# Expert layers of a top-2 mixture: tiles of 256 rows, with the first layer's weights as the stationary operand

## The reference, cut to what matters

```python
def _L1_ffn_ref(x, Wr, W1, b1, W2, b2):          # x: 32 x 96 x 192, F = 768, 8 experts
    x_flat = x.reshape(T, D)                     # T = 3072 rows
    gate_logits = x_flat @ Wr
    topw, topi = jax.lax.top_k(gate_logits, TOP_K)        # 2 of 8
    topw = jax.nn.softmax(topw, axis=-1)
    combine = jnp.zeros((T, N_EXPERTS), dtype=x.dtype)
    combine = combine.at[jnp.arange(T)[:, None], topi].add(topw)
    h = jax.nn.relu(jnp.einsum('td,edh->eth', x_flat, W1) + b1[:, None, :])
    y = jnp.einsum('eth,ehd->etd', h, W2) + b2[:, None, :]
    out = jnp.einsum('te,etd->td', combine, y)
    return out.reshape(B, S, D)
```

## Time and profile before

| what | value |
|---|---|
| time, median of 3 runs | 940.69 us (938.2 to 941.06) |
| span of the profiled execution | 938.0 us |
| the median less that span | 2.7 us |
| TensorE busy over the span | 770.3 us, 82% |
| VectorE / ScalarE / GpSimd busy | 553.9 / 424.6 / 362.2 us |
| first to last TensorE work of `expert_tiles` | 670.36 to 923.37 us |

### The profile page before, as it was taken

One profiled execution on the slowest core, in us unless ns is written; L12 is line 12 of the kernel. 1 busy time (PEld: TensorE's weight loads), 2 busy tenths in 40 slices (PEclk: granted clock), 3 DMA queues, 4 the chain that ended last, 5 costly groups with the idle time before them and its releaser, 6 DMA issues. The chain is left out here.

```text
span 938.0 us, 23848 instructions
## 1 busy us (share of the span) xinstructions
PE 770.3 (82%) x8368; PEld 648.7 (69%) x8369; DVE 553.9 (59%) x1400; ACT 424.6 (45%) x1069; POOL 362.2 (39%) x392
## 2 busy tenths in 40 slices
PE   3689999999977766556789999815599999999993
PEld 3578888888865543334557778604599999999993
DVE  2698887887742221111667777679555565556562
ACT  4667667677632211111125776445144444444441
POOL 1423434434320000000114788218755555555552
PEclk9999999999965987878669999855599999999997
DMA  9419000000026999999155000054123333333331
GB/s 256 111 47 429 33 2 2 2 2 3 2 102 194 422 423 426 426 425 396 28 237 240 1 2 1 1 146 103 59 45 53 50 54 50 49 49 49 53 50 17
DMA packets 34090, 118.16 MB, mean 126 GB/s; under 512 B 7570, under 2 KB 24372, under 8 KB 29524
## 3 DMA queue, kind: packets, MB, share of 16 engines
q1 hardware_dynamic: 23156, 104.30, 29.3%
q0 software_dynamic: 10848, 12.67, 8.4%
HBM read 105.77 MB, written 11.14 MB: 125 GB/s over the span
## 5 line engine op out<-in xcount | busy, mean ns | idle before, releaser
L1835 POOL DMA_INDIRECT out_h<-x_ys,idx x55 | 87.5, 1591 | 98.2 <-ACT x_ys L1860 93.2
L1959 PE MATMUL psum<-w_pairs,x_h_hi 128*128 x330 | 101.8, 371 | 1.2 <-DVE x_h_lo L1887 1.1
L1961 PE MATMUL psum<-w_pairs,x_h_lo 128*128 x330 | 82.6, 250 | 0.0
L1887 DVE TENSOR_TENSOR x_h_lo<-psum,x_h_hi 128x384 fp32r<-128x384 f32 x110 | 56.3, 553 | 39.0 <-ACT x_h_hi L1856 39.0
L521 POOL TENSOR_SCALAR a_u<-flat,a_mv 96x192 f32<-96x192 f32 x32 | 24.2, 757 | 133.9 <-DVE a_mv L693 133.9
L1860 ACT ACTIVATE x_ys<-x_ys,cw 128x192 f32<-128x192 f32 x55 | 25.1, 456 | 102.2 <-DVE x_ys L1898 102.2
L1856 ACT ACTIVATE x_h_hi<-psum 128x384 fp32r<-128x384 f32 x110 | 48.1, 489 | 37.6 <-PE psum L1948 35.8
L1959 PEld LDWEIGHTS psum<-w_pairs,x_h_hi 128*128 128x128 f32 x330 | 61.9, 188 | 3.5 <-issue 3.4
L1961 PEld LDWEIGHTS psum<-w_pairs,x_h_lo 128*128 128x128 f32 x330 | 62.9, 191 | 0.0
L1822 POOL DMA_INDIRECT x_xg<-xtab,idx x55 | 55.1, 1002 | 16.6 <-issue 16.1
L1208 PE MATMUL psum<-flat,yT 64*32 64x384 f32 x576 | 41.0, 639 | 24.9 <-issue 23.9
(11 more groups left out here) (284 smaller groups left out, 2264.8 us busy)
## 6 DMA issues: line engine op xcount, KB each, us to landing
flat<-in_slot_w SPq DMA_DIRECT2D x24, 2304.0 KB, 27.4
ring<-in_slot_w SPq DMA_DIRECT2D x8, 2304.0 KB, 29.7
flat<-in_moe_w SPq DMA_DIRECT2D x1, 10752.0 KB, 29.6
flat<-in_x_patches SPq DMA_DIRECT2D x4, 1536.0 KB, 14.2
out_h<-flat SPq DMA_DIRECT2D x1, 2304.0 KB, 12.1
xtab<-flat SPq DMA_DIRECT2D x4, 576.0 KB, 4.0
m_y<-in_fc_b SPq DMA_DIRECT2D x4, 384.0 KB, 7.4
x_xg<-xtab,idx POOLq DMA_INDIRECT x55
```

Source lines behind the costliest of these rows:

```text
L1835: pool.indirect_dma_start(out=A["out"][:, :], out_offset=bass.IndirectOffsetOnAxis(ap=g.idx[:, i:i + 1], axis=0), in_=ys[:, i % 2, :], in_ ...
L1887: v.tensor_tensor(h_lo[:, 3 * n:3 * n + 3, :], b_hT[n], h_hi[:, 3 * n:3 * n + 3, :].bitcast(F32), ALU.subtract).then_inc(s_hl, 1)
L1959: pe.matmul(b_y[u % 2], h_hi[:, k, :], g.w_pairs[:, :, k, bass.ds(e, 1), :].rearrange("p two a d -> p two (a d)"), start=(k == 0), stop=False)
L1961: mm = pe.matmul(b_y[u % 2][:, 1, :], h_lo[:, k, :], g.w_pairs[:, 1, k, bass.ds(e, 1), :].rearrange("p a d -> p (a d)"), start=False, stop ...
```

## The change

- `expert_tiles` takes 31 tiles of 256 rows (`NTB`), all of them always; a tile is two halves of 128 rows, so the lists have 62 columns (`NTILES`).
- In the first layer the weights are the stationary operand, a block of 128 features at a time, and x moves, 256 columns. So the features stand on the output's partitions, as the second layer needs them, and nothing is transposed in between. There are six groups `first(k)` of five matmuls, each into one of three PSUM banks, and six groups `second(k)`; they alternate.
- ScalarE makes relu's high part of a group, VectorE the low part in one scalar-tensor-tensor operation (`relu_rest`).
- The additions, the weighing and the scatters are done by halves. Scatters go ten halves behind the gathers; one waits for both halves of the tile before.
- The split first-layer weights no longer stay in SBUF for the products. attention1 stores them into a table in DRAM, `w1tab` (five DMAs, 12.4 MB, one of them of 62 partitions; `route` writes the bias rows), and SyncE fetches a tile's part, 1.573 MB, into one of four buffers, as soon as the first layer of the tile four before is done. The load of `b2` stands behind the first of them.

```diff
-NTILES = 55
+MT = 256
+NPAD = 256
+NWB = 4
+NTB = 31
+NTILES = 2 * NTB
...
+            for first, (low, high) in ((2, (2, 3)), (0, (0, 1))):
+                done = NE if first else 2 * NE
+                sp.wait_ge(g.s_hi, done)
+                sp.wait_ge(g.s_lo, done)
+                if first:
+                    sp.wait_ge(g.s_top, NE)
+                for m in (low, high):
+                    for rows in ((slice(0, 64), slice(66, 128)) if m == 3 else (slice(0, 128),)):
+                        sp.dma_start(A["w1tab"][:, rows, m * F:(m + 1) * F].rearrange("e p f -> p e f"),
+                                     g.w1_parts[m][rows, :, :].bitcast(F32)).then_inc(g.s_w1d, 16)
...
+            sp.wait_ge(g.s_w1d, 5 * 16)
+            sp.wait_ge(g.s_b1r, 32)
+            for i in range(NTB):
+                e = sp.value_load(g.te[0:1, i:i + 1], min_val=0, max_val=NE - 1)
+                if i >= NWB:
+                    sp.wait_ge(s_h1, (i - NWB + 1) * FC)
+                sp.dma_start(g.w1_buf[i % NWB].bitcast(F32), A["w1tab"][bass.ds(e, 1), :, :].rearrange("a p (m f) -> p (a m) f", m=4)
+                             ).then_inc(g.s_w1[i % NWB], 16)
+                if i == 0:
+                    sp.dma_start(b2[:, :, :], A["moe_b2"].unsqueeze(0).broadcast_to([128, NE, D])).then_inc(s_b2, 16)
...
-                i = t - 4
+                i = t - BEHIND
                 if i >= 0:
                     pool.wait_ge(s_ys, i + 1)
-                    if i >= 1:
-                        pool.wait_ge(s_add, 16 * i)
+                    if i >= 2:
+                        pool.wait_ge(s_add, 32 * (i // 2))
...
-            steps(act, NTILES, [(relu, 1), (x_copy, 0), (turn_copy, 1), (weigh, 2)])
+            steps(act, NTB, [(relu(0), 1), (relu(1), 1), (x_copy, 0), (weigh(0), 3), (relu(2), 1), (weigh(1), 3),
+                             (relu(3), 1), (relu(4), 1), (relu(5), 1)])
...
+            def relu_rest(k):
+                def stage(i, u):
+                    v.wait_ge(s_hh, i * FC + k + 1)
+                    v.scalar_tensor_tensor(h_lo[:, k, :], b_f[k % NF1], 0.0, h_hi[:, k, :].bitcast(F32),
+                                           ALU.max, ALU.subtract).then_inc(s_hl, 1)
+                return stage
...
-            steps(v, NTILES, [(relu, 1), (x_rest, 0), (turn_rest, 1), (add_bias, 2)])
+            steps(v, NTB, [(add_bias(0), 3), (relu_rest(0), 1), (relu_rest(1), 1), (x_rest, 0), (add_bias(1), 3),
+                           (relu_rest(2), 1), (relu_rest(3), 1), (relu_rest(4), 1), (relu_rest(5), 1)])
...
+            def first(k):
+                def stage(i, u):
+                    w = g.w1_buf[u % NWB]
+                    cols = slice(128 * k, 128 * k + 128)
...
+                    if not isinstance(i, int) or i * FC + k >= NF1:
+                        pe.wait_ge(s_hl, i * FC + (k + 1 - NF1))
+                    terms = ((x_hi, 0, 0, 128), (x_hi, 0, 1, 128), (x_lo, 0, 1, 128), (x_hi, 1, 2, 128), (x_lo, 1, 3, 66))
+                    for m, (x, c, part, rows) in enumerate(terms):
+                        mm = pe.matmul(b_f[k % NF1], w[0:rows, part, cols], x[0:rows, u % 2, c, :],
                                        start=(m == 0), stop=(m == len(terms) - 1))
                     mm.then_inc(s_h1, 1)
...
-            steps(pe, NTILES, [(pick, 0), (transpose_x, 0), (second, 2), (turn, 1), (first, 0)])
+            steps(pe, NTB, [(pick, 0), (first(0), 1), (second(0), 2), (first(1), 1), (second(1), 2), (transpose_x, 0),
+                            (first(2), 1), (second(2), 2), (first(3), 1), (second(3), 2), (first(4), 1), (second(4), 2),
+                            (first(5), 1), (second(5), 2)])
```

More of the change, by code:

```diff
@@ L178, in build @@
         g.s_add = sem("s_add")
+        g.s_w1d = sem("s_w1d")
+        g.s_w1 = [sem(f"s_w1_{i}") for i in range(NWB)]
         g.s_ring = [sem(f"s_ring{i}") for i in range(NU)]
@@ L1915, in expert @@
                 return pe.snap(regs[u], min_val=0, max_val=NE - 1)
[L1917 to L1918 removed]
             def transpose_x(i, u):
[L1921 to L1924 removed]
+                at = 2 * (u % 2)
+                for half in range(2):
+                    if isinstance(i, int):
+                        pe.wait_ge(s_x[at + half], 16 * (i // 2 + 1))
+                    else:
+                        pe.wait_ge(s_x[at + half], (i - u) * 8 + (16 * (u // 2) + 16))
@@ L1951, in second @@
-            def second(i, u):
-                if isinstance(i, int) and i == 0:
-                    pe.wait_ge(g.s_lo, n_early + len(on_pool))
-                    pe.wait_ge(s_lo_v, len(on_vector))
-                e = expert(u)
-                reused(pe, s_ya, i, 2)
-                for k in range(FC):
-                    pe.wait_ge(s_hl, i * 2 + k // 3 + 1)
-                    pe.matmul(b_y[u % 2], h_hi[:, k, :], g.w_pairs[:, :, k, bass.ds(e, 1), :].rearrange("p two a d -> p two (a d)"),
-                              start=(k == 0), stop=False)
-                    mm = pe.matmul(b_y[u % 2][:, 1, :], h_lo[:, k, :], g.w_pairs[:, 1, k, bass.ds(e, 1), :].rearrange(
-                        "p a d -> p (a d)"), start=False, stop=(k == FC - 1))
-                mm.then_inc(s_y, 1)
@@ L1965, in _, with second, stage @@
-            steps(pe, NTILES, [(pick, 0), (transpose_x, 0), (second, 2), (turn, 1), (first, 0)])
+                return stage
+            def second(k):
+                def stage(i, u):
+                    if isinstance(i, int) and i == 0 and k == 0:
+                        pe.wait_ge(g.s_lo, n_early + len(on_pool))
+                        pe.wait_ge(s_lo_v, len(on_vector))
+                    e = expert(u)
+                    if k == 0:
+                        reused(pe, s_ya, i, 2, 2)
+                    pe.wait_ge(s_hl, i * FC + k + 1)
+                    for half in range(2):
+                        part, bank = slice(128 * half, 128 * half + 128), b_y[u % 2][half]
+                        pe.matmul(bank, h_hi[:, k, part],
+                                  g.w_pairs[:, :, k, bass.ds(e, 1), :].rearrange("p two a d -> p two (a d)"),
+                                  start=(k == 0), stop=False)
+                        mm = pe.matmul(bank[:, 1, :], h_lo[:, k, part], g.w_pairs[:, 1, k, bass.ds(e, 1), :].rearrange(
+                            "p a d -> p (a d)"), start=False, stop=(k == FC - 1))
+                    mm.then_inc(s_y, 1)
+                return stage
```

202 lines of the change are left out of this document (93 added, 109 removed).

## The result

The changed kernel takes 958.45 us, the median of four runs (955.06 to 965.03), against 939.45 of the kernel before: a ratio of 1.0212 (1.0178 to 1.0246). That is 19 us slower, where 4 us faster had been forecast, and over the upper end of the range, 953. Each ratio in what follows is against executions of the kernel before that ran beside it, and leaves out executions over 1.5% slower than the fastest of the same kernel (three of ten in k1_store64, none elsewhere).

A forecast was written before the change was run, and what follows sets the result against it. The prediction took TensorE alone to pace the expert stage. Its terms, -13 us for TensorE, +7 up to the first matmul and +2 after the last, summed to -4: 936.7 us, with a range of 8 in 10 from 926 to 953.

The forecast's parts named there:

- TensorE, per tile: Expert stage: a tile of 256 rows takes 7.59 us, the stage 239.7 against 253.0, a gain of 13 us.
- rival B: First layer: matmuls of 256 columns run at the floor, 0.11 us each, 7 us better, 929; chance 0.17.
- the formula that the prediction quoted: Trainium skill, TensorE matmuls: columns / 2.4 GHz plus 2.5 ns, 109 ns at 256 columns; 8 us more gained, 929.
- the 0.20 for waits and the loop's edge: TensorE's tile in the expert stage: 0.20 us beyond matmuls and transposes, added unchanged to 7.39 to give 7.59.
- The tail: After the last matmul: two last scatters instead of one, one more issue with its gap, 1.9, taken as +2 us.
- rival D: VectorE in the expert stage: relu_rest queued behind other work delays TensorE, a tile at 7.9, +9 us, 946; chance 0.11.
- The front: Sorting stage up to the first matmul: longer list, extra cast, second gather and wider first operations, +7 us (bounds +5 and +9).
- counted as nothing: Attention stage: storing the split weights into DRAM, 12.4 MB, 29 us at 426 GB/s, was put at no cost.
- rival E: Weight stores to DRAM: 62 partitions on two engines make sorting-stage stores up to 19 us late; half, +9, 946; chance 0.10.
- list and cast: Sorting stage before the first gather: 62 list columns for 55 cost 2.7 us, a second cast on GpSimd 1.0.
- the term for the first weights beside the gathers: Before the first matmul: operations twice as wide and 6 MB of weights streaming beside the gathers, +1 to +2 us.
- rival C: GpSimd's scatter chain sets the expert stage's pace: cycle 6.8, slack 0.8, deciding from landings of 4.4; 955 with 5.0; chance 0.15.

The follow-up runs named there:

- k1_store64: The changed kernel with the DRAM store of 62 partitions made one of 64, bias rows written afterwards: ratio 1.0063 to the kernel before.
- k4_both: The changed kernel with the edits of k1_store64 and k2_paired together: ratio 0.9928 to the kernel before.
- k2_paired: The changed kernel with GpSimd issuing both gathers of a tile, then both scatters, instead of alternating: ratio 1.0024 to the kernel before.
- k3_loads4: The changed kernel with only the first four tiles loading first-layer weights, later tiles using what lies in the buffer: ratio 1.0008 to the kernel before.
- k5_loads_later: k4_both with b2 loaded first and the weight loads of tiles 1 to 3 waiting for the first two gathers: ratio 0.9944 to the kernel before.
- k7_casts_on_v: k5_loads_later with the row of ones and its two casts made by VectorE instead of GpSimd: ratio 0.9927 to the kernel before.

## Why the prediction was wrong

**TensorE, per tile: right in mechanism, too small in gain.** A group of the first layer and the two pairs of the second behind it, by start and length, in k4_both:

```profile
901.28 0.42 PE L1983 MATMUL psum<-x_x_hi,w_hi_ab 128*128 128x256 f32 x2
901.54 0.28 PE L1983 MATMUL psum<-x_x_lo,w_hi_ab 128*128 128x256 f32 x1
901.66 0.28 PE L1983 MATMUL psum<-x_x_hi,w_hi_ab 128*128 128x256 f32 x1
901.77 0.28 PE L1983 MATMUL psum<-x_x_lo,w_hi_ab 66*128 66x256 f32 x1
901.89 0.35 PE L1999 MATMUL psum<-w_pairs,x_h_hi 128*128 x1
...
902.45 0.42 PE L1983 MATMUL psum<-x_x_hi,w_hi_ab 128*128 128x256 f32 x2
```

901.89 - 901.28 = 0.61 for five matmuls, 0.122 for one, the upper bound of the prediction and not its floor, so rival B is out (and so are the 109 ns of the formula that the prediction quoted); 902.45 - 901.89 = 0.56 for the two pairs where 0.57 was used. Six times that and the four transposes of 0.44 make 7.46. The tile takes 7.42 and not 7.59 because the 0.20 for waits and the loop's edge, carried over from before, is not there. With both causes of delay removed the work takes 233.1 to 233.5 us, 20 less than before; 13 were forecast.

**The tail** was right: +2 forecast, +1.9 measured. **VectorE's order** (rival D) did not bind: without the scatters' delay there is no wait for `relu_rest` in k2_paired, k3_loads4 or k4_both. The operations of 256 columns took 0.42, less than the 0.475 used.

**The front: the step "counted as nothing" failed.** The stores to DRAM were put at nothing, with rival E at half of a bound and a chance of 0.10. Of the 20.6 us, 14.5 lie ahead of the first gather where 3.7 were forecast (list and cast), and 6.2 between the gather and the first matmul where 3.3 were. The mechanism of E was right, two engines and stores that come late, and its bound of 19 us was near: b1s came 20 us later than before, 3 of it drift, and the list lost 10.8 of them (k1_store64 gives 10.7 back). But the late piece was not a store of the sorting stage; it was a small load queued behind them, for which GpSimd waits ahead of its share of the sorting loop. The prediction did not ask what else stands in the queue that the slow store holds up. The other 2.9 us of the front, between the gather and the first matmul, are in the term for the first weights beside the gathers, put at +1 to +2: the second gather lands 6.82 us behind its issue where the first of before took 3.28. Their cause stays open (k5_loads_later, k7_casts_on_v).

**The scatters: the cycle of rival C lacked a term.** "A cycle of 6.8, slack 0.8" was the landing plus three issues. Between a landing and the start of the scatter that waits for it GpSimd takes some time of its own, which the profile calls issue. In the trace of before it stands in the chain of waits, in rows that the prediction did not use:

```profile
923.73 3.46 DMA out_h<-x_ys,idx
927.18 0.03 issue
...
927.23 0.71 issue
927.93 1.55 POOL out_h L1835
```

0.75 us from the landing at 927.18 to 927.93. The changed kernel's tail shows the same: a landing at 935.30, the next start at 936.05.

6.8 + 0.75 = 7.55, so the slack of 0.8 was not there, and the chain was a little slower than TensorE from the start: k3_loads4 measures 7.49 for 7.42. C's chance of 0.15 rested on that slack. The point from which it decides, put at landings of 4.4, was in truth at the usual landing of 3.5, and a load that meets a second scatter brings that to some 8 (8.4 to 9.3 from start to start, less 0.75).

**The chances.** C and E were given as alternatives, each with a time of its own around 950. They are independent, one ahead of the stage and one in it, and both came: -20 for TensorE, +19 for the stalls, +21 for the front, +2 for the tail, against the 25.1 less 3.0 of the profiled execution. The range held one mishap, not two. That C's own time, 955 with landings of 5.0, lies near the measured 958 is chance: landings were not 5.0 in every tile but long in three, and the front added as much.

## What to carry to other kernels

Before a DMA is counted as hidden, its number of partitions and what is issued behind it on the same queue are to be read: one slow transfer can hold up the later issues of that engine, however small (four of them took 6.4 to 25.1 us here), and the loss is where somebody waits for the smallest of them. A chain of transfers that wait for each other is costed from start to start, as the rows show it, with the time from a landing to the next start in it; and where such a chain is as long as the bound (7.49 for 7.42 here), its issues are to be ordered so that other work lies inside the landing, which won 18 us here with no byte and no wait changed. Rivals that touch different stages are added, not chosen between.

## What was not expected of the hardware

A stall of TensorE costs more than its idle time. In the changed kernel around the first stall (stretches, with the granted clock in the last column but two):

```profile
770.00:780.00 10.00, 10.00 (x80) 9.84 (x78) 4.26 (x12) 4.99 (x12) 5.15 (x4) 1.00 0.90 305
780.00:784.00 4.00, 0.13 (x2) 0.00 (x0) 0.98 (x4) 0.06 (x1) 0.36 (x1) 0.94 0.56 180
784.00:788.00 4.00, 3.88 (x17) 3.88 (x17) 2.43 (x8) 1.50 (x4) 3.39 (x3) 0.50 0.37 57
788.00:792.00 4.00, 4.00 (x25) 4.00 (x24) 0.85 (x2) 0.88 (x3) 2.28 (x3) 0.71 0.57 116
792.00:796.00 4.00, 4.00 (x34) 4.00 (x34) 3.13 (x9) 2.06 (x6) 3.29 (x3) 1.00 0.96 353
```

In the 4.0 us without work the clock falls from 1.00 to 0.50, and though TensorE is busy from 784.12 on, the full clock is back only within 788 to 792. The three stalls are 11.9 us of waiting, but their tiles lose 19; the other 7 lie in stretches like these, at the lower clock.
